# A hand-ordered decoder layer on one core: the order of its local-attention stage on five queues

## The reference

```python
# 1 local attention: 8 heads of 16, chunks of 12 queries, windows of 24 keys
matrix_ac = einsum('bnchd,bnkhd->bhnck', q_blocked, k_ctx)
matrix_bd = _rel_shift(einsum('bnchd,phd->bhncp', q_blocked, rel_k))   # relative positions
attn = softmax(tanh((matrix_ac + matrix_bd) / 50) * 50)
x += (attn @ v_ctx) @ Wpost.T
# 2 cross attention: 16 heads of 64, 512 context tokens, rotary keys
lat, ctx = layer_norm(x), layer_norm(context)
x += softmax(clip(q @ rope(k).T / 8, -11, 11)) @ v @ Wo + bo
# 3 mixture of 12 experts, top 3, two layers of weights with a gelu between
x += mixture2(gelu(mixture1(x)))
```

## Time and profile before

| | us |
|---|---|
| median of 3 runs (lowest, highest) | 462.17 (461.06, 462.23) |
| profiled execution, whole | 464.92 |
| its span, first to last instruction | 463.2 |
| PE busy in the span | 426.5 (92%) |
| VectorE, GpSimd, ScalarE busy | 341.2, 244.1, 196.6 |

### The profile page before, as it was taken

How to read it: one execution, slowest core, us unless ns; L and a number is a source line. 1 busy time by engine, 2 the same in 40 slices (tenths; PEclk the granted TensorE clock), 3 DMA queues, 4 the chain that set the end, 5 groups by cost and what they waited for, 6 DMA issues and landing times.

```text
span 463.2 us, 8468 instructions
## 1 busy us (share of the span) xinstructions
PE 426.5 (92%) x3168; PEld 312.6 (67%) x3168; DVE 341.2 (74%) x700; ACT 196.6 (42%) x312; POOL 244.1 (53%) x217
## 2 busy tenths in 40 slices
PE   3967889999999999998995998979989999999996
PEld 2645666766666776766772766748776788888885
DVE  8777747979998567987764688796995894564454
ACT  7747436556365345543433544432635642200000
POOL 5775228977799777976764554653432352000000
PEclk9999999999999999999997999988999999999999
DMA  7675305000000000000000000322645670000000
GB/s 182 168 162 79 81 6 94 0 1 0 1 1 2 0 2 1 0 1 1 1 2 0 2 1 0 139 47 46 142 63 130 137 155 13 7 6 7 11 6 13
DMA packets 75434, 19.85 MB, mean 43 GB/s; under 512 B 66741, under 2 KB 73834, under 8 KB 75394
## 3 DMA queue, kind: packets, MB, share of 16 engines
q1 hardware_dynamic: 73636, 18.65, 18.8%
q10 hardware_dynamic: 1758, 0.65, 0.7%
HBM read 17.27 MB, written 2.02 MB: 42 GB/s over the span
## 4 chain that ended last, share of the span: by engine, by line
PE 66%; DVE 9%; ACT 5%; issue 4%; POOL 1%; DVEq 0%; ACTq 0%; POOLq 0%
PE psum L1155 11%; PE psum L1138 8%; PE psum L948 7%; PE psum L1335 5%; PE psum L1336 5%; PE psum L1334 5%; PE psum L1298 4%; PE psum L1300 4%; PE psum L1299 4%; PE psum L1174 3%; PE psum L1165 3%; PE psum L1057 2%; ACT e_sb L774 2%; DVE rden L1557 1%; DVE x_sb L1516 1%
## 5 line engine op out<-in xcount | busy, mean ns | idle before, releaser
L529 POOL TENSOR_TENSOR e_part<-e_sb 128x512 f32<-128x512 f32 x64 | 88.6, 1401 | 52.2 <-DVE e_sb L1550 39.1
L774 ACT ACTIVATE e_sb<-psum 128x1024 f32<-128x1024 f32 x64 | 62.2, 1022 | 21.0 <-PE psum L1138 21.0
L1155 PE MATMUL psum<-e_sb,v_sb 128*64 128x256 f32 x512 | 64.6, 393 | 0.8 <-ACT v_sb L682 0.8
L1138 PE MATMUL psum<-q_t,kT 64*128 64x256 f32 x512 | 64.2, 389 | 0.0
L1752 DVE SCALAR_TENSOR_TENSOR x_sb<-psum,dw,x_sb 128x128 f32<-128x128 f32 x96 | 33.7, 351 | 36.9 <-PE psum L1336 34.3
L1550 DVE TENSOR_SCALAR e_sb<-e_sb 128x1024 f32<-128x1024 f32 x64 | 53.1, 862 | 5.5 <-ACT e_sb L774 5.5
L754 ACT ACTIVATE kT<-psum 128x512 f32<-128x512 f32 x32 | 19.2, 599 | 89.4 <-PE psum L1057 89.1
L1557 DVE RECIPROCAL rden<-psum 128x256 f32<-128x256 f32 x32 | 55.9, 1746 | 0.3 <-PE psum L1165 0.2
L1138 PEld LDWEIGHTS psum<-q_t,kT 64*128 64x128 f32 x512 | 46.7, 186 | 9.7 <-issue 5.3
L563 POOL TENSOR_TENSOR xeT_lo<-xeT,xeT_hi 128x512 fp32r<-128x512 f32 x24 | 30.9, 1290 | 40.5 <-ACT xeT_hi L788 38.0
L1155 PEld LDWEIGHTS psum<-e_sb,v_sb 128*64 128x64 f32 x512 | 34.9, 139 | 23.5 <-issue 7.1
(11 more groups left out here) (194 smaller groups left out, 783.8 us busy)
## 6 DMA issues: line engine op xcount, KB each, us to landing
w_raw<-in_L_ffn_W_dram SPq DMA_DIRECT2D x96, 64.0 KB, 2.3
gates<-gate_dram SPq DMA_DIRECT2D x6, 768.0 KB, 4.7
ctx_sb<-in_ctx_dram SPq DMA_DIRECT2D x4, 256.0 KB, 5.7
vbd<-v_dram SPq DMA_DIRECT2D x16, 52.6 KB
v_dram<-v_tok SPq DMA_DIRECT2D x4, 136.0 KB, 3.1
raw<-in_L_xattn_Wkv_dram SPq DMA_DIRECT2D x2, 256.0 KB, 4.7
k_rot<-in_L_xattn_Wkv_dram SPq DMA_DIRECT2D x2, 256.0 KB, 4.6
k_rot<-in_L_xattn_Wq_dram SPq DMA_DIRECT2D x2, 256.0 KB, 5.2
```

What stands on the lines that cost most here:

```text
L529: pool.tensor_tensor(e_part[:, p % 2, half, :, :], e_sb[:, i % ERING, :, 0, :], e_sb[:, i % ERING, :, 1, :], ALU.add)\
L774: act.activation(e_sb[:, i % ERING, :, :, :].rearrange("p a k t -> p (a k t)"), psum[:, a:a + 2, :].rearrange("p a b -> p (a b)"), ACT.Exp ...
L1138: mm = pe.matmul(psum[:, 2 * (i % 2) + a, t * S:(t + 1) * S], kT[rows, p % 3, kt * P:(kt + 1) * P], q_t[rows, j % 2, p % 2, :], start=True ...
L1155: mm = pe.matmul(psum[DX * a:DX * a + DX, pv_bank(p), 0:S], v_sb[g % 2][:, kt, 2 * pp + a, :], e_sb[:, i % ERING, a, t, :], start=(kt == 0 ...
```

## The change

No computation is added or removed. Calls change places on all five queues:

- SP/ACT: the four DMAs of `store_positions` for half 1 move from SP to ACT; ACT issues them right behind its last `positions_out`.
- ACT: the context of sequence 0 is copied ahead of position chunks 3 to 5; three of the last shifted reads and `local_softmax(0)` are put in another order; `value_unit(9)` comes later.
- PE: `turn_context(0)` goes ahead of `relative(3..5)`, into bank 7; `unit(9)` goes from between `local_values(2)` and `(3)` to ahead of `queries(0)`; `turn_keys(2)` goes ahead of `local_project(3)`; `unit(10)` and its wait for x1_done go behind `scores(2)`, `scores(3)` of round 0.
- VectorE: `context_lo(0)` goes into the middle of the second mask products `kM`, the sign of sin ahead of them; the context statistics are spread out; `key_unit(7)` goes ahead of the position additions of chunks 3 to 5; `latents_lo(0)` ahead of `context_normalize(1)`.
- POOL: `key_sum(0..3)` are mixed with `weight_rest(2..3)`; `weight_rest(4..5)` go behind.

```diff
+        def store_positions(queue, half):
+            queue.wait_ge(s["bd_raw_done"], HCH * (half + 1))
...
+                queue.dma_start(bd_dram[i:WALL:WG][ks].rearrange("k q r -> q k r"), bd_raw[QT * i:QT * i + QW, ks, :])\
+                     .then_inc(s[f"bd_stored{half}"], 16)
@@ sync
-            store_positions(0)
+            store_positions(sp, 0)
...
-            store_positions(1)
@@ gpsimd
-            for n in range(6):
-                weight_rest(n)
-            for k in range(KC):
-                key_sum(k)
+            weight_rest(0)
+            weight_rest(1)
+            key_sum(0)
+            key_sum(1)
+            weight_rest(2)
+            key_sum(2)
+            weight_rest(3)
+            key_sum(3)
...
+            weight_rest(4)
+            weight_rest(5)
@@ scalar
-            for c in range(HCH, NCH):
-                positions_out(c)
...
-                act.activation(ctx_f[:, :], bank(6 if b == 0 else MISC_BANK), ACT.Identity, scale=affine[:, 2:3], bias=affine[:, 3:4])\
+                act.activation(ctx_f[:, :], bank(7 if b == 0 else MISC_BANK), ACT.Identity, scale=affine[:, 2:3], bias=affine[:, 3:4])\
...
             context_f(0)
+            for c in range(HCH, NCH):
+                positions_out(c)
+            store_positions(act, 1)
...
-            for i in range(3):
+            for i in range(2):
                 shift_positions(act, 1, i)
             value_unit(4)
+            shift_positions(act, 1, 2)
+            local_softmax(0)
+            value_unit(5)
             shift_positions(act, 1, 3)
-            value_unit(5)
-            local_softmax(0)
             local_softmax(1)
...
-            value_unit(9)
...
             outputs_turned(3)
+            value_unit(9)
@@ tensor
-                    pe.wait_ge(s["bd_raw_done"], 4)
+                    pe.wait_ge(s["bd_raw_done"], 3)
...
+            turn_context(0, 7, "ct_ps")
             for c in range(HCH, NCH):
                 relative(c)
-            turn_context(0, 6, "ct_ps")
...
             local_values(2)
-            unit(9)
             local_values(3)
...
             turn_outputs(3)
+            unit(9)
             queries(0)
...
             local_project(2)
+            turn_keys(2)
             local_project(3)
-            pe.wait_ge(s["x1_done"], NT)
-            unit(10)
-            turn_keys(2)
...
                     scores(2 * r + 3)
+                if r == 0:
+                    pe.wait_ge(s["x1_done"], NT)
+                    unit(10)
@@ vector
+                    if j and g == 2:
+                        context_lo(0)
...
-            context_lo(0)
-            dve.wait_ge(s["ld_rope"], 32)
-            dve.tensor_scalar(sin_sb[:, :, 0, :], sin_sb[:, :, 1, :], -1.0, None, ALU.mult).then_inc(s["sin_done"], 1)
+                    dve.wait_ge(s["ld_rope"], 32)
+                    dve.tensor_scalar(sin_sb[:, :, 0, :], sin_sb[:, :, 1, :], -1.0, None, ALU.mult).then_inc(s["sin_done"], 1)
...
+            context_statistics(1)
             for c in range(HCH):
                 add_positions(c)
-            for b in range(1, B - 1):
-                context_statistics(b)
             key_unit(6)
+            key_unit(7)
             for c in range(HCH, NCH):
                 add_positions(c)
-            key_unit(7)
+            context_statistics(2)
...
+            latents_lo(0)
             context_normalize(1)
-            latents_lo(0)
```

More of the change, by code:

```diff
@@ L342, in decoder_layer @@
         BIAS = {10: ("turn", 0), 11: ("product", 0), 13: ("turn", 1), 14: ("product", 1)}
+        def store_positions(queue, half):
+            queue.wait_ge(s["bd_raw_done"], HCH * (half + 1))
+            ks = half_groups(half)
+            for i in range(WG):
+                queue.dma_start(bd_dram[i:WALL:WG][ks].rearrange("k q r -> q k r"), bd_raw[QT * i:QT * i + QW, ks, :])\
+                     .then_inc(s[f"bd_stored{half}"], 16)
         def shift_positions(queue, half, i):
```

## The result

The changed kernel runs in 457.98 us (median of 22 runs, 454.37 to 461.97), the kernel before beside it in 462.01 us (22 runs, 460.27 to 465.32). The ratio is 0.9896 with a 95% interval of 0.9875 to 0.9916, which is 4.8 us of 462. The ratio leaves out three of the changed kernel's 22 runs (461.28, 461.28 and 461.97 us), which count as slow; the medians of all runs lie 4.0 us apart. The profiled execution of the changed kernel has a span of 456.1 us, 7.1 less than that of before.

The account below looks back on a forecast made before the run. How early PE, nearly pauseless in the rounds, reaches them was taken to bound the kernel. Gains 2.9 + 1.4 + 1.1 = 5.4, less 0.4 for hand-offs, give 5.0: 462.17 to 457.2 us, range 455.6 to 460.9.

Parts of the forecast that it names:

- Part 1: SP's queue: four store issues fewer save 2.14 us, spreads start at 29.3, shifted reads land at 33.5.
- Part 2: Early context on PE, ACT and VectorE: the pieces only change places, worth 0.
- Part 3: POOL's key sums ahead of weight rests: key units 2 and 3 on VectorE run 2.3 us sooner.
- Part 4: VectorE and ACT before the local stage: additions at 33.8, local_values(0) at 39.7, local_project(0) at 45.0.
- The first gain: Start of the first projection: local_project(0) at 45.0 for 47.95, 2.9 us gained.
- The values: Local stage: local_values(2) up to 1.1 us late at worst, waiting for SP's spreads; taken as 0.
- Part 5: Latents and queries: latents move 2.9 us sooner; filling PE's wait with unit(9) keeps full clock, 1.4 us or nothing.
- Part 6: Entry into the rounds on PE: waits of 1.55 and 0.65 us go, 1.1 lost before unit(11); gain 1.1.
- (a): Rival: clock stays low at the queries or falls at a new pause; 458.6 us, chance 0.22.
- (b): Rival: DMA transfers, not issues, bind, so shifted reads land no sooner; 458.9 to 460.3 us, chance 0.15.
- (c): Rival: PE's early saving returns as waits in rounds 0 to 3; 461.5 us, chance 0.08.
- (d): Rival: ACT stops waiting for its own stores, making it slower; 464.4 us if they land at 38, chance 0.05.

Follow-up runs that it names:

- e2: Changed kernel with POOL's old order, six weight rests ahead of the first key sum; ratio 0.9954 to the kernel before.
- e3: Changed kernel with VectorE's old order around the position additions (context statistics behind them, key_unit(7) last); ratio 0.9933 to the kernel before.
- e4: Changed kernel with unit(10), its wait for x1_done and turn_keys(2) back ahead of round 0; ratio 0.9941 to the kernel before.
- e5: Changed kernel with unit(9) and value_unit(9) back between local_values(2) and (3); ratio 0.9871 to the kernel before.
- e8: Kernel before with only the four stores of half 1 issued by ACT, behind positions_out(5); ratio 1.0027 to the kernel before.
- e9: Changed kernel again without any edit, for a second profile; ratio 0.9886 to the kernel before.
- e10: Changed kernel with the context late again on PE, ACT and VectorE, stores still on ACT behind it; ratio 0.9911 to the kernel before.
- e1: Changed kernel with the four stores of half 1 given back to SP, behind the value stores; ratio 0.9941 to the kernel before.
- e12: Kernel before with only POOL's new order and VectorE's new order around the position additions; ratio 0.9986 to the kernel before.
- e7: Changed kernel with four of the eight shifted reads of half 0 issued by ACT; ratio 0.9886 to the kernel before.
- e6: Changed kernel with four of the eight shifted reads of half 0 left out; ratio 0.9895 to the kernel before.
- e11: Changed kernel with unit(9) and value_unit(9) at their old place and four half 0 reads on ACT; 455.89 us, ratio 0.9859 to the kernel before.

## Why the prediction was right, point by point

The sum, 5.0 us, came out at 4.8. Of its terms some were right by themselves and some by balance. The pair of profiles shows 5.0 us at exponent 12, made up otherwise than I had it: 2.1 us at the start of the queries (I had 2.9), 1.5 by the clock behind them (1.4), 1.8 by the entry (1.1), and 0.4 lost between scores(0) and the end of the local stage. That the total agrees so well is luck: the entry gave 0.7 too much about where the values wait took 0.8 away.

**Part 1, SP.** I took 2.14 us off SP, as if each issue kept its duration. In the first profile the remaining issues stretched by more than that; in the second the spreads started at 28.84, even ahead of the forecast 29.3. Over all profiles the step holds in the mean: the eight with the stores on ACT and eight reads on SP (changed, e2, e3, e4, e5, e8, e9, e10) have the start between 28.4 and 32.1, at 30.2 in the mean; the three with the stores on SP (before, e1, e12) between 31.4 and 33.3, at 32.5 in the mean. That is 2.3 us apart. What failed is the forecast of a single profile. The lag of the last read behind its issue, 4.3 us, was one sample too: it was 3.0 in the changed kernel's first profile (31.57 to 34.60), and in e9, where the last issue ended at 28.73, additions at 32.79 were not waiting at all.

**Part 2, the context, priced at 0.** Key unit 0 came at 26.2, 1.0 us sooner than forecast. Two things make it up: sin took 0.21 us and not 1.33 (below), and unit(0) was ready early. e10, with a short sin (0.22) but the context late, has VectorE wait 1.01 us for unit(0) and start at 27.05. What lets ACT do four stores without delaying the key units is that the context stands ahead of them, early or late: behind them it costs 2.3 us (e8), ahead of them and late 0.8 (e10). As a price for the whole the 0 stands within the error (e10).

**Part 3, POOL.** The timeline came 0.85 us ahead of the forecast (key unit 2 at 29.05 for 29.9, with 0.21 us of wait), since key unit 0 did. What I did not see is that ACT's stores would have made the old order worse by 2.6 us (e2). I wrote that `weight_hi` 1.6 us late was hidden; it is hidden only by this part.

**Part 4, VectorE and ACT.** Forecast: local_values(0) at 39.7, local_project(0) at 45.0. Measured 40.15 and 44.64, and 38.63 and 43.87 in e9. The first gain, 2.9 us, came as 3.3 and 4.1. e3 shows what VectorE's order has to do with it: without it `local_project(0)` came at 46.82, although SP was as early as in e9.

**The values: the term that was wrongly put at nothing.** I had `local_values(2)` up to 1.1 us late and priced it at 0, because the latents did not depend on it. In the first profile it was 1.11 us late, and it counted: VectorE's `local_normalize(2)`, which waits for these products, stands ahead of the second latent step in VectorE's order. lat_lo came at 53.72, 2.1 us sooner than 55.82, where 3.3 had been gained at the projection. The other profiles bear it out: from `local_project(0)` to lat_lo it takes 7.9 us in before, e1, e7, e9 and e10, where `local_values(2)` does not wait for `vbd`, 9.1 in the changed kernel and e6 with waits of 1.11 and 1.01, and 9.7 in e4 with 1.61. An engine's queue ties two chains that no data ties.

**Part 5, the clock.** Forecast 1.4 us if the clock stayed up, and in the pair of profiles it came: from queries(0) to scores(0) PE took 3.55 us before (56.30 to 59.85) and 2.08 after (54.20 to 56.28), 1.5 us. The reason I gave is wrong: in e5 the wait is unfilled and the clock stays. The term also leaned on one profile of before: e8 and e12, with PE's order of before, have no half clock there, so that it counted in this pair is luck. The Trainium skill (TensorE: Matmul & The Clock Gate, What's actually happening) has activity release the throttle; the traces show both levels, but e5's unfilled 1.20 us at 1.00 shows that one short wait does not decide it. With a low clock elsewhere (e3), the same sort of loss came back at another place.

The change may still raise the clock on the average. The runs list the mean granted clock of each: it is 0.985 over the 72 runs of before that stand beside the experiments, 0.989 over the changed kernel's 22, 0.988 in e12, and 0.984, 0.984, 0.983 and 0.984 in e1, e2, e3 and e8. Runs at 0.992 or 0.993 alone have spans of 458.8 us in the mean (ten of before) and 454.7 (eleven of the changed kernel), 4.1 apart. So most of the gain is there at equal clock, and some of it, and of what e1 to e3 lose, comes through the clock; which wait does it was not tried.

**Part 6, the entry.** Priced at 1.1, measured 1.8: waits of 1.10, 0.65 and 0.45 gone, 1.06 new, as laid out, which gave 1.3 by exponent 8, and 0.5 more in round 4 that I had not looked for.

**Rivals.** (a) The clock fell neither at the queries nor ahead of unit(11) in the changed kernel. (b) Transfers instead of issues: partly so in e6, where issues came earlier and the values did not. The Trainium skill (DMA: Bandwidth & Descriptors, Issuing engines are not separate DMA queues) allows a second issuer only the issue time as a gain; e7, which moved four issues without a measurable gain, is no contradiction, and in e1 the stores cost more than their own issue time of 1.99 us in one place: they stand ahead of the reads that VectorE waits for. (c) Nothing was eaten: from exponent 12 to exponent 44 all kernels take 120.2 us (120.22 before, 120.17 after). (d) ACT's wait for the stores did not show, its reads began at 30.17; but e8 shows the neighbour of that rival, ACT's issues holding up what is queued behind them, at 1.2 us.

**The rest of the 7.1 us between the two spans.** 5.0 us are there at exponent 12. The other 2.1 lie where the kernels are the same: 1.0 between exponents 44 and 56 (53.13 us and 52.17, with mean clocks of 0.94 and 0.93; the other profiles have 52.2 to 53.4), and 1.0 behind that, where stretches at half clock differ. Late in the rounds before had 11 us at a mean of 0.69, after 4 us at 0.57, and e9 a full clock:

```profile
305.00:316.00 11.00, 8.51 (x34) 5.71 (x31) 10.03 (x14) 3.09 (x6) 5.83 (x5) 0.69 0.40 66
```
```profile
305.00:309.00 4.00, 4.00 (x14) 3.26 (x13) 3.31 (x5) 2.39 (x5) 2.52 (x2) 0.57 0.11 20
```
```profile
300.00:310.00 10.00, 8.52 (x53) 7.20 (x52) 8.41 (x14) 4.09 (x7) 3.79 (x3) 1.00 0.37 61
```

From exponent 56 to the first gelu this makes 77.75 us, 76.72 and 75.15; with unrelated edits e7 had 77.70 and e2 75.12. That goes with the execution and with none of the edits, and it is why the runs show 4.0 to 4.8 us and not the 7.1 of this pair.

## What to carry to other kernels

Price a DMA issue as a range, not as the one duration of the profile, and take a second profile before a difference of 1 to 3 us in a start time is explained. That holds for the profile of before too: a stretch at half clock that one profile shows may be gone in the next. When work is moved to another engine, follow what is queued behind it through the next engine too: here the stores on ACT alone cost 1.2 us, and with the context ahead of them and POOL's sums ahead of its rests they gained some 2 (±1.8). A chain that is free in data can still be tied by an engine's order: look at what stands ahead of it in the queue.

## What the runs showed of the hardware

The sign of sin, one VectorE instruction over 128x128 elements, took 1.33 us in the kernel before, while POOL worked on a weight rest, and 0.21 us after, while POOL waited. In e12 it stands at its old place, but POOL waits there, and it takes 0.22. Before, after and e12:

```profile
25.86 1.33 DVE L1451 TENSOR_SCALAR sin_sb<-sin_sb 128x128 f32<-128x128 f32 x1
```
```profile
21.26 0.21 DVE L1460 TENSOR_SCALAR sin_sb<-sin_sb 128x128 f32<-128x128 f32 x1
```
```profile
26.35 0.22 DVE L1457 TENSOR_SCALAR sin_sb<-sin_sb 128x128 f32<-128x128 f32 x1
```

POOL's rows meanwhile: busy from 25.82 before; idle from 20.7 to 27.66 after. In both profiles with a long sin (before, and e8 with 1.33 as well) it starts 0.04 to 0.05 us behind a POOL weight rest of 1.29 us and ends 0.08 to 0.09 us behind that one's end, which looks like waiting for that one instruction. `rope_a`, which reads one operand from PSUM, takes 0.69 us beside POOL's rests in before and 0.69 without them after. What in POOL's work does it was not tried. The issue of four value stores by SP, the same instructions in all kernels, took from 2.41 us (e9) to 4.22 us (e8). Nearly all of that is one issue: the fourth store takes 0.48 to 0.52 us in e2, e3, e5, e9, e10 and e11, and 1.27 (before) to 2.21 us (changed) in the others; in e8 it is the third, with 1.93. In before, e1 and e12 ACT issues no DMA at that time, so ACT's issues are not what it takes. What holds that issue was not found.
